# FFN rows transposed by VectorE, normalised by GpSimd, silu on ScalarE, and another order of products at the end of a pair of blocks

## The chip, the cores and the metric

One core of one Trainium2 chip runs the whole program. The metric is the device time of one execution in microseconds; the time of a kernel is the median of its runs.

## The reference

A gated cross-attention block and a gated feed-forward block, each with a residual. x is 2 x 1024 x 512, the context 2 x 77 x 512, there are 16 heads of 32, and the FFN has 1536 hidden units with integer weights scaled by 1/127.

```python
def _silu(x):
    return jax.nn.silu(x)

def _L0_ffn_ref(x, w_gate, w_up, w_down):
    wg = _dequant(w_gate, x.dtype)
    wu = _dequant(w_up, x.dtype)
    wd = _dequant(w_down, x.dtype)
    gate = jnp.einsum('bsd,hd->bsh', x, wg)
    up = jnp.einsum('bsd,hd->bsh', x, wu)
    h = _silu(gate) * up
    return jnp.einsum('bsh,dh->bsd', h, wd)

x = x + jnp.tanh(g_xattn[0]) * _L0_xattn_ref(_layernorm(x, axis=-1), ctx_1024, ctx_1024, ...)
x = x + jnp.tanh(g_ffn[0]) * _L0_ffn_ref(_layernorm(x, axis=-1), ...)
```

## The kernel before, in words

The 2048 rows are eight blocks of 512. A first stage does the attention block by block and stores x_mid in HBM; GpSimd builds beside it the weights' variants w_var (four sums and three plain quarters per slice of 128 hidden units), which go to HBM too. The second stage, to which the change belongs, is the FFN. It takes the blocks in four pairs, p = 0 to 3.

A pair has twelve slots, m = 0 to 11, one per slice of hidden units. In a slot gate and up of both blocks of the pair come from seven products instead of eight (a scheme of Strassen's kind): the quarters A of the weights stand against the quarters B11, B21, B22 and the differences T1 to T4 of the transposed, normalised rows. Each product is 4 matmuls (`strassen`, L1880), since every row variant is held as a rounded part and a remainder (xv[:, j, 0] and xv[:, j, 1]). The slot's weights lie in a ring of three (`load_w`, L385). ScalarE takes three snapshots of partial sums (`snap1`, `snap2`, `snap3`, L973 to L985) and two tanh (L991, L998); VectorE forms the gate and up of both blocks (`gate2`, `upper1`, `upper2`, L1421 to L1456), completes silu by (tanh + 1) x gate (`silu1`, `silu2`, L1435 and L1441) and multiplies (`hidden1`, `hidden2`, L1448 and L1463). ScalarE then rounds the hidden values (`h_high`, L1005) and GpSimd writes the remainder (`h_low`, L705, first th1, then c12).

The down projection (`down`, L1930) of six slots runs behind slot m = 6 for the first half and behind the last slot for the second. One tile of rows takes 12 matmuls, six slots x two parts, and the eight tiles of a pair alternate between two PSUM banks; VectorE adds each to acc (`result`, L1471) and so frees the bank. In `pair` of TensorE the last slot's p4 and p3 and parts of the first two tiles stand before the rest.

The rows of the next pair are prepared during a pair. SyncE loads x2 in four parts in slots 0 to 3 (L361). VectorE takes statistics (`stats2`, L1257) between the first half's results and normalises there (`normalise2`, L1265); GpSimd computes the standard deviations (L654, L656). At the pair's end TensorE transposes the rows in four groups of eight (`turn`, L1704) into PSUM; from there ScalarE and VectorE form B11 to B22 and T1 to T4 (`xv_copy`, `form`, `xv_low`) and GpSimd the remainders of T1 to T4 (L663). For pair 0 the same happens at the end of the attention, where GpSimd normalises (L682).

Every engine runs its own list in the order in which it is written; semaphores tie the lists. An engine that waits holds up all that is behind it in its list. The order of the FFN is in the five functions named `pair`, one per engine. VectorE also takes the maximum of the ring's weights (`largest_gu`, L1476), in slots 0 to 5 of pair 0 and 6 to 11 of the last pair; it decides at the end whether an exact slow path has to run, which it does not here.

## Time and profile before

| | us |
|---|---|
| median of 3 runs | 872.54 |
| lowest and highest | 872.40, 872.73 |
| the profiled execution | 872.86 |
| its span, first to last instruction | 871.0 |

The profile is of one execution. Its span is 1.9 us shorter than the time of the same execution. A timeline row gives the start, the duration of the group, the engine, the line and the operands; an idle time before the group and what ended it stand in brackets. PE is TensorE, DVE VectorE, ACT ScalarE, POOL GpSimd. A matmul's own duration (some 390 ns) overlaps with its neighbours', so the spacing of starts tells what one costs.

### The profile page before, as it was taken

The page shows a single profiled execution, that of the slowest core. Times are in us where ns is not written, and L with a number is a line of the kernel's source. Part 1 is how long each engine was busy: PE and PEld are TensorE (multiplying, and loading weights), DVE is VectorE, ACT ScalarE, POOL GpSimd, SP SyncE. Part 2 cuts the span into 40 slices and gives each one's busy share as a digit, 9 for nine tenths or more (in the row PEclk, how much of TensorE's full clock was granted, in tenths as well). Part 3 has the DMA queues.
Part 4 walks back from the last instruction along what each step waited for, and adds up shares of the span by engine and source line. Part 5 has one row for each costly group of instructions (what it writes and reads, how often), then busy time and mean ns, then how long its engine had stood idle before and what let it go on. Part 6 is the DMA issues. An engine that isn't in the chain of part 4 may idle for free.

```text
span 871.0 us, 12870 instructions
## 1 busy us (share of the span) xinstructions
PE 855.0 (98%) x4087; PEld 706.8 (81%) x4087; DVE 653.3 (75%) x1081; ACT 461.1 (53%) x1130; POOL 403.1 (46%) x344
## 2 busy tenths in 40 slices
PE   8999999999999999999999999999999999999997
PEld 6678888888888887888888888888888888888876
DVE  5988877777786878679688478788487887587882
ACT  5787575756666757546056265165363364461550
POOL 4664555555565665437144444155253256151250
PEclk9999999999999999999999999999999999999999
DMA  9233847272728131567333256043275143243202
GB/s 329 78 107 121 270 153 253 84 241 85 242 97 277 48 133 38 212 234 266 116 120 135 97 187 248 14 165 122 74 247 187 48 164 107 96 171 117 90 38 98
DMA packets 60406, 128.73 MB, mean 148 GB/s; under 512 B 7616, under 2 KB 20416, under 8 KB 60352
## 3 DMA queue, kind: packets, MB, share of 16 engines
q1 hardware_dynamic: 58960, 125.95, 41.9%
q10 hardware_dynamic: 1392, 2.10, 0.7%
q8 instruction: 29, 0.48, 0.2%
q14 instruction: 25, 0.20, 0.1%
HBM read 99.93 MB, written 27.79 MB: 147 GB/s over the span
## 4 chain that ended last, share of the span: by engine, by line
PE 86%; DVE 6%; ACT 3%; issue 1%; DMA 1%; POOL 1%; ACTq 0%; DVEq 0%
PE psum L1880 34%; PE psum L1591 20%; PE psum L1930 18%; PE psum L1660 9%; PE psum L1616 4%; DMA xs<-x_t 1%; PE psum L1704 1%; ACT e L800 1%; POOL hT L705 1%; DVE bn L1055 1%; DVE K L1149 1%; DVE mx L1105 1%; DVE e L1097 0%; DVE qT L1079 0%; DVE mx L1094 0%
## 5 line engine op out<-in xcount | busy, mean ns | idle before, releaser
L1880 PE MATMUL psum<-xv,ring 128*128 128x512 f32 x1344 | 308.0, 390 | 1.0 <-ACT a L985 0.7
L1880 PEld LDWEIGHTS psum<-xv,ring 128*128 128x128 f32 x1344 | 251.3, 188 | 55.1 <-ACT a L985 1.1
L705 POOL TENSOR_TENSOR hT<-th,hT 128x512 fp32r<-128x512 f32 x48 | 86.7, 1806 | 200.7 <-ACT hT L1005 200.7
L1930 PE MATMUL psum<-w_d,hT 128*128 128x512 f32 x768 | 177.7, 390 | 1.3 <-POOL hT L705 0.8
L1930 PEld LDWEIGHTS psum<-w_d,hT 128*128 128x128 f32 x768 | 143.6, 188 | 32.7 <-POOL hT L705 2.0
L554 POOL TENSOR_TENSOR e<-e,rden 128x616 f32<-128x616 f32 x64 | 78.0, 1219 | 110.4 <-DVE rden L1131 75.2
L800 ACT ACTIVATE e<-psum,nmx,q_scale 128x77 f32<-128x77 f32 x256 | 102.9, 428 | 3.1 <-DVE nmx L1111 3.1
L973 ACT ACTIVATE a<-psum 128x512 f32<-128x512 f32 x48 | 28.7, 599 | 131.6 <-PE psum L1880 131.4
L1471 DVE SCALAR_TENSOR_TENSOR acc<-psum,gate_ffn,acc 128x512 f32<-128x512 f32 x64 | 47.6, 749 | 65.1 <-PE psum L1930 65.1
L1660 PE MATMUL psum<-wo,aT 128*128 128x512 f32 x384 | 95.5, 398 | 0.5 <-DVE aT L1079 0.5
L1591 PE MATMUL psum<-xT,wq 128*128 128x512 f32 x360 | 89.1, 398 | 0.4 <-DVE qT L1079 0.4
L1660 PEld LDWEIGHTS psum<-wo,aT 128*128 128x128 f32 x384 | 69.8, 188 | 14.3 <-DVE aT L1079 0.8
L1591 PEld LDWEIGHTS psum<-xT,wq 128*128 128x128 f32 x360 | 65.5, 188 | 14.7 <-DVE qT L1079 1.9
L705 POOL TENSOR_TENSOR hT<-c,hT 128x512 fp32r<-128x512 f32 x48 | 62.3, 1297 | 22.2 <-ACT hT L1005 22.2
L1591 PE MATMUL psum<-pT,V 128*128 128x512 f32 x288 | 68.0, 392 | 0.6 <-DVE aT L1079 0.6
L773 ACT ACTIVATE pT<-psum 128x512 fp32r<-128x512 f32 (+1 forms) x96 | 49.7, 534 | 33.9 <-PE psum L1616 33.9
L1591 PE MATMUL psum<-K,qT 128*128 128x308 f32 x384 | 63.9, 310 | 0.9 <-ACT e L800 0.9
L1591 PEld LDWEIGHTS psum<-pT,V 128*128 128x128 f32 x288 | 53.3, 188 | 12.5 <-DVE aT L1079 1.1
L1435 DVE SCALAR_TENSOR_TENSOR th<-th,c 128x512 f32<-128x512 f32 x48 | 56.1, 1168 | 7.1 <-ACT th L998 4.3
L1591 PEld LDWEIGHTS psum<-K,qT 128*128 128x128 f32 x384 | 56.9, 188 | 5.4 <-ACT e L800 1.8
L1005 ACT ACTIVATE hT<-th 128x512 fp32r<-128x512 f32 x48 | 30.4, 633 | 54.2 <-DVE th L1448 54.2
L1068 DVE TENSOR_TENSOR pT<-psum,pT 128x512 fp32r<-128x512 f32 (+1 forms) x96 | 55.7, 588 | 2.6 <-ACT pT L773 0.9
(110 smaller groups left out, 1204.7 us busy)
## 6 DMA issues: line engine op xcount, KB each, us to landing
ring<-w_var SPq DMA_DIRECT2D x48, 896.0 KB, 4.6
w_var<-stage SPq DMA_DIRECT2D x12, 896.0 KB, 4.6
x_ln<-x SPq DMA_DIRECT2D x32, 256.0 KB, 4.7
x_res<-x SPq DMA_DIRECT2D x32, 256.0 KB, 5.2
x_mid<-x_res SPq DMA_DIRECT2D x32, 256.0 KB, 2.0
x<-x_mid SPq DMA_DIRECT2D x16, 512.0 KB, 5.6
acc<-x_mid SPq DMA_DIRECT2D x16, 512.0 KB, 6.2
out<-acc SPq DMA_DIRECT2D x32, 256.0 KB, 2.0
```

What stands on the lines that cost most here:

```text
L554: nc.gpsimd.tensor_tensor(e[:, t % 2, hs], e[:, t % 2, hs], rden[:, t % 2, hs].unsqueeze(2).to_broadcast([P, UH, SK]), ALU.mult).then_inc( ...
L705: nc.gpsimd.tensor_tensor(hT[:, 1, i % HH, j, :], h[:, :], hT[:, 0, i % HH, j, :].bitcast(f32), ALU.subtract).then_inc(h_lo, 1)
L773: nc.scalar.activation(dst, src, ACT.Copy).then_inc(t_hi, 1)
L800: last = nc.scalar.activation(e[:, t % 2, UH + h, :], s_bank[1][:, h // HG, (h % HG) * SK:(h % HG + 1) * SK], ACT.Exp, bias=nmx[:, t % 2, ...
L1068: nc.vector.tensor_tensor(dst, src, hi.bitcast(f32), ALU.subtract).then_inc(t_free, 1)
L1435: nc.vector.scalar_tensor_tensor(th2[:, :], th2[:, :], 1.0, c22[:, :], ALU.add, ALU.mult)\
L1471: nc.vector.scalar_tensor_tensor(acc[:, t, :], m_bank[t % 2][:, :], gate_ffn[:, 0:1], acc[:, t, :], ALU.mult, ALU.add).then_inc(m_free, 1)
L1591: last = nc.tensor.matmul(dst, stat, mov, start=(j == 0), stop=(j == len(terms) - 1))
L1616: last = nc.tensor.transpose(t_bank[at % 2][:, j * P:(j + 1) * P], rows[:, start:start + P], ident[:, :])
L1660: last = nc.tensor.matmul(m_bank[t % 2][:, :], aT[:, a, m, t * P:(t + 1) * P], wo[:, c, m, :], start=m == 0 and a + c == 0, stop=m == G - ...
L1880: last = nc.tensor.matmul(psum[:, bank, :], stat, mov, start=start and j == 0, stop=j == len(terms) - 1, skip_group_check=not start)
L1930: last = nc.tensor.matmul(m_bank[t % 2][:, :], hT[:, a, m, t // TT, (t % TT) * P:(t % TT + 1) * P], w_d[:, HH * h + m, :], start=m == 0 an ...
```

## The change

Rows and their transposition: for pairs 1 to 3 SyncE loads all four parts of x2 at once, for pair 1 before the last block of the attention is stored, for pairs 2 and 3 at the start of the pair before. VectorE takes the statistics in slots 1 to 4, GpSimd normalises behind its subtractions of slots 3 and 4, and VectorE transposes the rows in 32 operations per pair (`turn_rows`), each of sixteen 32 x 32 squares, from x2 to two new buffers x2_t0 and x2_t1 in SBUF. Of these, 2 stand in slot 5, 2 in slot 6, 20 between the first half's results, 8 in slots 7 to 9. T1 and T3 are formed in slots 10 and 11, T2 and T4 between the second half's results. T1 to T4 take the place of x2. Pair 0 is prepared as before, with TensorE.

silu is one operation on ScalarE, ACT.Silu in the place of ACT.Tanh; VectorE's `silu1` and `silu2` are gone, and so is the factor 0.5 in the gate.

The end of a pair on TensorE: tile 0's slots 0 to 3, p4, tile 1's, p3, tile 2's, then slot 4 of all three, slot 5 of all three, then tiles 3 to 7. Tile 2 is summed in a bank of the gate and up products (set_c[0]). The ring's maxima are all taken in the last pair. The buffer causal moves to a region of the attention, 32 elements are put in front of the ring, and region_b grows.

```diff
-            b12 = sb("b12", [P, KH, TB], f32, b2)
-            sb("gap2", [P, 2 * G * GK + 2 * NV * P - PT * D - KH * TB], f32, b2)
+            x2_t1 = sb("x2_t1", [P, KD, TB], f32, b2)
+            sb("gap2", [P, ALIGN], f32, b2)
             ring = sb("ring", [P, 3, 7, KH, P], f32r, b2)
+            x2_t0 = sb("x2_t0", [P, KD, TB], f32, b2)
...
+        formed_rows = x2[:, :, :].rearrange("p (v k) n -> p v k n", v=TT)
+        b11, b21 = x2_t0[:, 0:KH, :], x2_t0[:, KH:KD, :]
+        b12, b22 = x2_t1[:, 0:KH, :], x2_t1[:, KH:KD, :]
...
+                if rows_ahead:
+                    sp.wait_ge(xb_full, nth(TURNED, 0, B21))
+                    for j in range(TT):
+                        load_x2(1, j)
...
+                if 0 < p < NP - 1:
+                    sp.wait_ge(xv_lo, nth(LO_ORDER, p, T4))
+                    for j in range(TT):
+                        load_x2(p + 1, j)
                 for m in range(MH):
                     i = MH * p + m
                     sp.wait_ge(p3_full, i + 1)
-                    if p == 0 and m < HH:
-                        sp.wait_ge(w_max_done, m + 1)
...
-                    if p + 1 < NP and m < TT:
-                        sp.wait_ge(xb_full, nth(TURNED, p, B21))
-                        load_x2(p + 1, m)
...
+                    if p + 1 < NP and m in (2, 4):
+                        rstd_ahead(2 * p + 1 + m // 2)
+                        mean_ahead(2 * p + 1 + m // 2)
+                    if p + 1 < NP and m in (3, 4):
+                        normalise(2 * p - 1 + m)
                 if p + 1 < NP:
-                    variants_low(p + 1)
+                    for j in LO_ORDER:
+                        xv_low(p + 1, j, j)
...
+            def xv_round(q, j):
+
+                full, half_of = {B11: (b11, 0), B21: (b21, 0), B22: (b22, 1)}[j]
+                act.wait_ge(x2_turned, turned(half_of, q))
+                act.wait_ge(last_use(j), MH * q)
...
-                nc.scalar.activation(th1[:, :], psum[:, set_a[i % 2], :], ACT.Tanh, scale=0.5 * W_SCALE)\
-                    .then_inc(tanh1_done, 1)
-
-            def tanh2(i):
+                nc.scalar.activation(th1[:, :], psum[:, set_a[i % 2], :], ACT.Silu, scale=W_SCALE)\
+                    .then_inc(silu1_done, 1)
...
-                    xv_copy(p + 1, B11, b11_at)
-                tanh2(last)
-                tanh1(last)
+                    xv_round(p + 1, B11)
+                silu2(last)
+                silu1(last)
                 if more:
-                    b12_copy(p + 1)
+                    xv_high(p + 1, T1)
                 h_high(last, 0)
+                if more:
+                    xv_round(p + 1, B21)
                 h_high(last, 1)
                 if more:
-                    xv_high(p + 1, T1)
-                    xv_copy(p + 1, B21, b21_at)
+                    xv_high(p + 1, T3)
                     xv_high(p + 1, T2)
-                    xv_high(p + 1, T3)
                     xv_high(p + 1, T4)
-                    b22_copy(p + 1)
+                    xv_round(p + 1, B22)
...
-            def normalise2(i, tiles=range(TT)):
-                dve.wait_ge(rstd2_ready, i + 1)
-                for t in tiles:
-                    at = TT * (i % 2) + t
-                    nc.vector.tensor_scalar(x2[:, at, :], x2[:, at, :], mv2[:, at, 0:1], rstd2[:, at:at + 1],
-                                            ALU.subtract, ALU.mult).then_inc(x2_normed, 1)
+            def turn_rows(q, half_of, ops):
+
+                tiles = slice(TT * half_of, TT * half_of + TT)
+                dve.wait_ge(x2_normed, PT * q + TT * (half_of + 1))
+                if q > 1:
+                    dve.wait_ge(xb_lo, nth(XB_ORDER, q - 1, B22))
+                for op in ops:
+                    a, c = divmod(op, HG)
+                    rows = x2[a * HD:(a + 1) * HD, tiles, :].rearrange("p t (k n) -> p t k n", n=P)
+                    to = x2_t[half_of][c * HD:(c + 1) * HD].rearrange("p k (t n) -> p t k n", n=P)
+                    nc.vector.transpose(to[:, :, :, a * HD:(a + 1) * HD], rows[:, :, :, c * HD:(c + 1) * HD])\
+                        .then_inc(x2_turned, 1)
...
+                    one, other = b12, b11 if q else pair_of(b11_at)
                 if j == T2:
-                    dve.wait_ge(xb_full, nth(TURNED, q, B22))
-                    dve.wait_ge(v_formed, nth(FORMED, q, T1))
-                    ins = nc.vector.tensor_tensor(lo, pair_of(b22_at), xy[:, T1, 1], ALU.subtract)
+                    one, other = b22 if q else pair_of(b22_at), variant(q, T1)
                 if j == T3:
-                    ins = nc.vector.tensor_tensor(lo, pair_of(b22_at), b12[:, :, :], ALU.subtract)
+                    one, other = b22 if q else pair_of(b22_at), b12
                 if j == T4:
-                    dve.wait_ge(xb_full, nth(TURNED, q, B21))
-                    dve.wait_ge(v_formed, nth(FORMED, q, T2))
-                    ins = nc.vector.tensor_tensor(lo, pair_of(b21_at), xy[:, T2, 1], ALU.subtract)
-                ins.then_inc(v_formed, 1)
+                    one, other = b21 if q else pair_of(b21_at), variant(q, T2)
+                nc.vector.tensor_tensor(variant(q, j), one, other, ALU.subtract).then_inc(v_formed, 1)
...
-            def silu2(i):
-
-                dve.wait_ge(tanh2_done, i + 1)
-                nc.vector.scalar_tensor_tensor(th2[:, :], th2[:, :], 1.0, c22[:, :], ALU.add, ALU.mult)\
-                    .then_inc(silu2_done, 1)
-
-            def silu1(i):
-
-                dve.wait_ge(tanh1_done, i + 1)
-                nc.vector.scalar_tensor_tensor(th1[:, :], th1[:, :], 1.0, psum[:, set_a[i % 2], :],
-                                               ALU.add, ALU.mult).then_inc(silu1_done, 1)
...
+            FILL = (4, 6, 8, 11, 13, 16, 18, 21, 24)
+
             def first_half(p, more):
                 for t in range(PT):
-                    if more:
-                        stats2(2 * p + 2 + t // TT, t % TT)
-                    elif t < HH:
+                    if not more and t < HH:
                         dve.wait_ge(rd_used, HH)
                         largest(MH + t, w_d[:, 2 * t:2 * t + 2, :].bitcast(f32).rearrange("p m d -> p (m d)"))
                     result(p, 0, t)
-                    if more and t >= PT - 2:
-                        normalise2(2 * p + 2, range(2 * (t - PT + 2), 2 * (t - PT + 2) + 2))
-                if more:
-                    normalise2(2 * p + 3)
+                    if more:
+                        turns(p + 1, range(FILL[t], FILL[t + 1]))
...
-                        silu2(i - 1)
-                        silu1(i - 1)
                         hidden1(i - 1)
                         upper2(i - 1)
                         hidden2(i - 1)
-                    if p == 0 and m < HH or p == NP - 1 and m >= HH:
+                    if p == NP - 1:
                         largest_gu(i)
+                    if more and 1 <= m <= TT:
+                        for t in (2 * m - 2, 2 * m - 1):
+                            stats2(2 * p + 2 + t // TT, t % TT)
+                    if more and m in (HH - 1, HH):
+                        turns(p + 1, range(2 * (m - HH + 1), 2 * (m - HH + 2)))
+                    if more and HH < m < HH + 4:
+                        at = (24, 27, 30, 32)[m - HH - 1:m - HH + 1]
+                        turns(p + 1, range(at[0], at[1]))
+                    if more and m == MH - 2:
+                        form(p + 1, T1)
+                    if more and m == MH - 1:
+                        form(p + 1, T3)
                 gate2(last)
-                silu2(last)
                 if more:
                     xv_low(p + 1, B11, b11_at)
-                silu1(last)
                 hidden1(last)
                 upper2(last)
                 hidden2(last)
                 if not more:
                     widest()
-                if more:
-                    form(p + 1, T1)
                 result(p, 1, 0)
                 result(p, 1, 1)
+                result(p, 1, 2)
                 if more:
                     form(p + 1, T2)
-                    form(p + 1, T3)
-                result(p, 1, 2)
-                if more:
                     xv_low(p + 1, B21, b21_at)
-                    form(p + 1, T4)
                 result(p, 1, 3)
                 if more:
+                    form(p + 1, T4)
+                result(p, 1, 4)
+                if more:
                     xv_low(p + 1, B22, b22_at)
-                for t in range(4, PT):
+                for t in range(5, PT):
...
+                    if (h, t) == (1, 2):
+                        pe.wait_ge(c12_done, MH * p + MH - 1)
+                    else:
+                        m_wait(i)
                 h_lo = (h1_lo, h2_lo)[t // TT]
                 for m in slots:
-                    if t % TT == 0:
+                    if t in (0, 1, 2, TT):
...
-                if more:
-                    turn(p + 1, B11)
-                    turn(p + 1, B12)
+                early, late = range(HH - 2), range(HH - 2, HH - 1)
+                down(p, 1, 0, early)
                 p4(last)
+                down(p, 1, 1, early)
                 p3(last)
-                down(p, 1, 0, range(HH - 1))
-                down(p, 1, 1, range(HH - 1))
+                down(p, 1, 2, early)
+                for t in range(3):
+                    down(p, 1, t, late)
                 if not more:
                     pe.wait_ge(w_top_done, 1)
                     pe.wait_ge(c11_done, last)
                     nc.tensor.transpose(psum[0:1, set_b[0], 0:P], w_top[:, :], ident[:, :]).then_inc(w_top_row, 1)
-                down(p, 1, 0, range(HH - 1, HH))
-                down(p, 1, 1, range(HH - 1, HH))
-                if more:
-                    turn(p + 1, B22)
-                    turn(p + 1, B21)
-                for t in range(2, PT):
+                for t in range(3):
+                    down(p, 1, t, range(HH - 1, HH))
+                for t in range(3, PT):
                     down(p, 1, t)
```

## Rows read from the trace of the kernel before

**Rows 1.** The page's part 1: engine, busy us, share of the span, instructions.
```profile
PE 855.0 (98%) x4087; PEld 706.8 (81%) x4087; DVE 653.3 (75%) x1081; ACT 461.1 (53%) x1130; POOL 403.1 (46%) x344
```

**Rows 2.** The chain that ended last, FFN: start us, us, engine, line, count.
```profile
372.00 42.81 PE psum L1880 x188
...
436.58 31.75 PE psum L1880 x140
...
496.02 42.75 PE psum L1880 x188
```

**Rows 3.** Timeline, end of pair 0: start us, us, engine, line, out<-in, count [idle before].
```profile
468.16 1.91 PE L1704 MATMUL psum<-ident,x 128*128 128x128 f32 x16
...
471.74 4.70 PE L1930 MATMUL psum<-w_d,hT 128*128 128x512 f32 x20
...
474.84 1.81 POOL L705 TENSOR_TENSOR hT<-th,hT 128x512 fp32r<-128x512 f32 x1 [3.75 <-ACT hT L1005]
...
476.70 1.20 PE L1930 MATMUL psum<-w_d,hT 128*128 128x512 f32 x4 [0.26 <-POOL hT L705]
...
477.73 1.91 PE L1704 MATMUL psum<-ident,x 128*128 128x128 f32 x16
...
495.85 4.37 PE L1880 MATMUL psum<-xv,ring 128*128 128x512 f32 x18
```

**Rows 4.** Timeline, end of the last pair.
```profile
837.76 2.43 PE L1880 MATMUL psum<-xv,ring 128*128 128x512 f32 x10
...
847.97 1.17 PE L1930 MATMUL psum<-w_d,hT 128*128 128x512 f32 x4
...
848.84 1.41 DVE L1471 SCALAR_TENSOR_TENSOR acc<-psum,gate_ffn,acc 128x512 f32<-128x512 f32 x2
...
849.64 16.61 PE L1930 MATMUL psum<-w_d,hT 128*128 128x512 f32 x72 [0.50 <-DVE acc L1471]
```

**Rows 5.** Timeline of pair 0 around the first-half down projection.
```profile
409.87 0.68 DVE L1430 TENSOR_TENSOR c<-psum,a 128x512 f32<-128x512 f32 x1
...
410.60 1.30 POOL L705 TENSOR_TENSOR hT<-c,hT 128x512 fp32r<-128x512 f32 x1 [0.61 <-ACT hT L1005]
...
414.65 21.93 PE L1930 MATMUL psum<-w_d,hT 128*128 128x512 f32 x96
```

**Rows 6.** Groups by line and form: out<-in, count | busy us, mean ns | idle before.
```profile
L705 POOL TENSOR_TENSOR hT<-th,hT 128x512 fp32r<-128x512 f32 x48 | 86.7, 1806 | 200.7 <-ACT hT L1005 200.7
...
L1660 PE MATMUL psum<-wo,aT 128*128 128x512 f32 x384 | 95.5, 398 | 0.5 <-DVE aT L1079 0.5
...
L1591 PE MATMUL psum<-pT,V 128*128 128x512 f32 x288 | 68.0, 392 | 0.6 <-DVE aT L1079 0.6
...
L705 POOL TENSOR_TENSOR hT<-c,hT 128x512 fp32r<-128x512 f32 x48 | 62.3, 1297 | 22.2 <-ACT hT L1005 22.2
...
L1435 DVE SCALAR_TENSOR_TENSOR th<-th,c 128x512 f32<-128x512 f32 x48 | 56.1, 1168 | 7.1 <-ACT th L998 4.3
...
L1441 DVE SCALAR_TENSOR_TENSOR th<-th,psum 128x512 f32<-128x512 f32 x48 | 32.5, 676 | 1.2 <-ACT th L991 1.2
...
L1257 DVE BATCH_NORM_STATS2 bn<-x 128x6 f32<-128x512 f32 x32 | 21.9, 684 | 0.0
...
L1265 DVE TENSOR_SCALAR x<-x,mv,rstd 128x512 f32<-128x512 f32 x24 | 11.4, 541 | 0.0
...
L711 POOL CAST w_d<-raw_d 128x1024 fp32r<-128x1024 int32 x6 | 8.9, 1505 | 0.0
...
L656 POOL TENSOR_TENSOR rstd<-rstd,half 128x4 f32<-128x4 f32 x8 | 8.4, 1051 | 0.7
...
L682 POOL TENSOR_SCALAR x<-x,nmean,rstd 128x512 f32<-128x512 f32 x8 | 6.1, 773 | 0.0
...
L654 POOL TENSOR_SCALAR rstd<-mv 128x4 f32<-128x4 f32 x8 | 1.6, 194 | 53.2 <-DVE mv L1259 53.2
...
L750 ACT ACT_TABLE_LOAD x1 | 1.3, 1283 | 4.6 <-issue 4.6
```

More of the change, by code:

```diff
@@ L69, in flamingo_gated_block @@
     FIRST = (2, 3, 0, 1)
+    ALIGN = 32
     PT = 2 * TT
@@ L330, in xv_low_ready, with formed, variant, rounded @@
                 eng.wait_ge(xv_lo, nth(LO_ORDER, q, j))
-        def xv_parts(j):
-            return xv[:, j, 0], xv[:, j, 1], xy[:, j, 1]
+        def formed(q, j):
+            return nth((T1, T3, T2, T4) if q else FORMED, q, j)
+        def variant(q, j):
+            return formed_rows[:, FORMED.index(j)] if q else xy[:, j, 1]
+        def rounded(q, j):
+            return nth((B11, T1, B21, T3, T2, T4, B22) if q else HI_ORDER, q, j)
+        def last_use(j):
+            return {B11: p1_full, B21: p2_full, T4: p4_full, T1: p5_full, T2: p6_full, T3: p7_full, B22: p3_full}[j]
         def pair_of(bank):
             return psum[:, bank:bank + 2, :]
+        TURNS = HG * HG
+        def turned(half, q):
+            return TURNS * (2 * (q - 1) + half + 1)
+        def down_bank(h, t):
+            return psum[:, set_c[0], :] if (h, t) == (1, 2) else m_bank[t % 2][:, :]
         block = ctx.enter_context(nc.Block())
@@ L386, in load_w, with residual @@
                     .then_inc(w_in[i % 3], 16)
-            def residual(n, first=False, ahead=False, keeps=((), ())):
+            def residual(n, first=False, ahead=False, keeps=((), ()), rows_ahead=False):
                 for t in range(TT):
@@ L658, in xv_low, with mean_ahead, normalise @@
             def xv_low(q, j, unread):
-                hi, lo, full = xv_parts(j)
-                pool.wait_ge(xv_hi, nth(HI_ORDER, q, j))
-                pool.wait_ge(v_formed, nth(FORMED, q, unread))
-                nc.gpsimd.tensor_tensor(lo, full, hi.bitcast(f32), ALU.subtract).then_inc(xv_lo, 1)
-            def variants_low(q):
-                xv_low(q, T1, T2)
-                xv_low(q, T3, T3)
-                xv_low(q, T2, T4)
-                xv_low(q, T4, T4)
-            def mean_first(i):
-                c = slice(TT * i, TT * i + TT)
+                pool.wait_ge(xv_hi, rounded(q, j))
+                if not q:
+                    pool.wait_ge(v_formed, nth(FORMED, 0, unread))
+                nc.gpsimd.tensor_tensor(xv[:, j, 1], variant(q, j), xv[:, j, 0].bitcast(f32), ALU.subtract)\
+                    .then_inc(xv_lo, 1)
+            def mean_ahead(i):
+                c = slice(TT * (i % 2), TT * (i % 2) + TT)
                 nc.gpsimd.tensor_scalar(nmean2[:, c], mv2[:, c, 0], -1.0, 0.0, ALU.mult, ALU.add).then_inc(nmean_ready, 1)
-            def normalise_first(i, tiles):
+            def normalise(i, tiles=range(TT)):
                 pool.wait_ge(nmean_ready, i + 1)
@@ L1271, in form @@
+            def form(q, j):
+                if q:
+                    dve.wait_ge(x2_turned, turned(1, q))
+                else:
+                    if j == T1:
+                        dve.wait_ge(b12_kept, 1)
+                    dve.wait_ge(xb_full, nth(TURNED, 0, {T1: B11, T2: B22, T3: B22, T4: B21}[j]))
+                if j == T2:
+                    dve.wait_ge(v_formed, formed(q, T1))
+                if j == T4:
+                    dve.wait_ge(v_formed, formed(q, T2))
                 if j == T1:
-                    dve.wait_ge(b12_kept, q + 1)
@@ L1492, in widest, with turns @@
                 nc.vector.tensor_copy(wide[:, :], wide_f[:, :]).then_inc(wide_ready, 1)
+            def turns(q, ops):
+                for half_of in range(2):
+                    inside = [op - TURNS * half_of for op in ops if op // TURNS == half_of]
+                    if inside:
+                        turn_rows(q, half_of, inside)
+            FILL = (4, 6, 8, 11, 13, 16, 18, 21, 24)
             def first_half(p, more):
                 for t in range(PT):
-                    if more:
-                        stats2(2 * p + 2 + t // TT, t % TT)
-                    elif t < HH:
+                    if not more and t < HH:
                         dve.wait_ge(rd_used, HH)
@@ L1851, in last_step @@
                 o(3, range(G))
-                turn(0, B11)
-                turn(0, B12)
+                turn(B11)
+                turn(B12)
                 p(n, 3, 1)
@@ L1867, in _ @@
                 if m == 1:
-                    turn(0, B22)
-            turn(0, B21)
+                    turn(B22)
+            turn(B21)
             pe.wait_ge(m_free, M_LAST + 4)
```

141 lines of the change are left out of this document (62 added, 79 removed).

## Prediction

> **What bounds the kernel now.** I read the page first: TensorE is busy for 98% of the span, VectorE for 75, GpSimd for 46 [rows 1]. So only what TensorE executes, and what makes it pause, can move the time. Next the chain of work that ended last, in order of time [rows 2]: from 372 us it is the FFN, four pairs of blocks, and inside a pair it is only TensorE. The 140 matmuls of the second half take 31.75 us, 0.2268 us each. A pair holds 336 matmuls of the seven-product scheme and 192 of the down projection, 528 x 0.2268 = 119.75 us, but it lasts 496.02 - 372.00 = 124.02 us. These 4.27 us are what the change can reach per pair. The timeline of the pair's end shows them [rows 3]. Sixteen transposes start at 468.16; the 8 matmuls behind them take 1.81, and the down projection starts at 471.74: 1.77 us for the transposes. Of its first 24 matmuls the last four start only at 476.70, released by GpSimd's subtraction of 474.84, so the group ends at 477.73 instead of 477.18: 0.55 us. Sixteen more transposes follow, and the 72 matmuls left (16.33) end at 495.85: 1.79 us. That is 4.11; 0.16 is left over. The last pair has no transposes, but it waits [rows 4]: its seventh product ends at 837.76 + 10 x 0.2268 = 840.03, and 32 matmuls later (7.26) it should be at 847.29, where the row says 849.64: 2.35 us of waits, on ScalarE's snapshot, on VectorE's gate sum (delayed by a maximum of the ring), and on the first result that frees a bank.
>
> **The change, part by part.** TensorE's transposes leave pairs 0 to 2: 3 x 3.56 = 10.7 us off the path.
>
> The new pair end. TensorE now does 8 down matmuls, p4, 8, p3, 8, then slot 4 (6 matmuls) and slot 5 (6) for three rows of tiles at once. The snapshot for p4 has 1.81 us of matmuls over it where the last pair waited; the gate sum for p3 the same and more. Slot 5 is first wanted 38 matmuls or 8.6 us after the seventh product; before it was wanted 4 matmuls ahead of 477.18, 8.1 us after it. VectorE's two fused multiplies are gone from silu, one of them 1168 ns [rows 6], so the last subtraction comes earlier too. I cost the old waits (0.55 in pairs 0 to 2, 2.35 in the last) at nothing. What is late next is the bank: tile row 3 needs the bank of tile row 1, and thus the second result. In [rows 4] the first result starts 848.84 - 847.97 = 0.87 us behind the first closing product, and two take 1.41. So the bank is free at 2.28, and the six matmuls are done at 1.36: a wait of 0.92, plus a restart (four matmuls from 476.70 take 1.03 to the next start, not 0.91 [rows 3]): 1.04 us in all four pairs. The last has one small transpose more, 0.1.
>
> Normalising on GpSimd. Eight operations a pair of 773 ns [rows 6] go in order between the subtractions that the down projection waits for. In pair 0 of before the second subtraction of slot 4 ends at 410.60 + 1.30 = 411.90, and the down projection starts at 414.65 and wants slot 5 eleven matmuls in, at 416.92 [rows 5]. Now GpSimd has the standard deviation (0.19 + 1.05), the mean (0.19) and about 0.1 between them, 1.5 us, and four normalisations, 3.05, ahead of slot 5's first subtraction: it starts at 416.45 and, at the 1297 ns of the undisturbed form [rows 6], ends at 417.75. TensorE waits 0.85 and restarts for 0.12: 1.0 us in pairs 1 and 2. In pair 0 the six conversions of 1505 ns stand in the same queue in slots 0 to 2; GpSimd works them off except for about 0.45, so 1.4 us there. That is 3.4 us in all. Slots 3 and 4 are split late as well; the silu that waits for that reuse of its buffer stands more than half a slot (3.2 us) behind, so I take nothing.
>
> Turning rows on VectorE. 32 operations a pair of 512 elements on 32 partitions; no row of before shows one. From below, a plain pass over 512 elements costs 541 ns; from above, an engine that fills a block and drains it before the next would need two passes, about 1.2 us. I take the statistics' 684 ns [rows 6], one element at a time in one stream, which it is nearest to. VectorE loses 12 x (1168 + 676) ns of silu a pair [rows 6], 22 us, and gets 32 x 0.69 = 22. Twenty of the 32 stand between the eight results of the first half, at 0.7 a result [rows 4]: 20 x 0.69 + 8 x 0.7 = 19.4 us under 96 matmuls, 21.77 us. They fit, so nothing. In the slots with three of them VectorE comes to the gate sum about 1 us late; it now ends at 410.55 where its product starts 12 matmuls before the down projection, at 411.93 [rows 5], 1.4 us later. Nothing. The forming of four variants reads SBUF instead of PSUM at about the same 1.2 us each, and the first variants are formed before the pair ends, so they are ready sooner than now, where the next pair starts without a wait [rows 2, 3].
>
> SyncE. The four 512 KB loads of rows leave the slots and stand ahead of the pair's ring loads, four issues; for pair 1 they stand ahead of the stores of the attention, which start later than they do. The ring is three slots deep, two of them (56 matmuls, 12.7 us) are in hand. Nothing. The ring's maxima of pair 0 move to the last pair, 1.2 us in a slot that has lost 1.8.
>
> ScalarE computes silu instead of tanh: same count and size. One load of a table, 1283 ns [rows 6], must come before the first silu. It costs from nothing, in ScalarE's idle time (busy 53% [rows 1]), to all of its 1.3 us; nearer the first, 0.2. The trace of before shows that one load was enough for Copy, Exp and Tanh. The Trainium skill (ScalarE: Activation LUTs, What ACT_TABLE_LOAD costs) gives about 2.66 us with the drain for a switch of set; by that the sum would be up to 1.4 us higher, as an estimate; the trace of before shows the load alone.
>
> Placement. By the sizes in the code the ring and the row variants stay at equal places modulo 256 bytes, as before; V and pT, equal before, come to lie 128 bytes apart. No row shows unequal operands of this kind. The 288 matmuls with V take 236 ns each, those with Wo, equal too, 249 [rows 6]; the difference bounds a gain or a loss at 288 x 13 ns = 3.7 us. I take nothing.
>
> **Sum.** Pair 0: 4.27 - 0.16 - 1.4 - 1.04 = 1.7. Pairs 1 and 2: 4.11 - 1.0 - 1.04 = 2.1 each. Last pair: 2.35 - 1.14 = 1.2. Less 0.2: 6.9 us. The profiled execution took 872.86 us (span 871.0 and 1.9 around it) and so comes to 866.0; the median of the runs is 0.3 lower, so 865.7.
>
> **Rivals.**
> 1. GpSimd is not late (its queue keeps ahead, or the stretch between has more room than I give it): the 3.4 us come back, 862.3. For it: GpSimd is busy 46% only [rows 1]. Against it: the order of the queue.
> 2. Turns somewhat dearer, 0.8 to 0.95 us: above 0.8 the first half's VectorE work passes 21.77 us and each 0.1 costs 2 us a pair. 866 to 874.
> 3. The slower side: turns at 1.2 us. Twenty and the results need 29.6 us, 7.8 over, in three pairs 23.5: about 889. It decides from 0.92 us a turn, where 3 x 2.3 us eat the gain. For it: nothing in the trace says that blocks overlap. Against it: the one-source rows of 512 elements lie between 0.54 and 0.77 [rows 6].
> 4. Placement costs the whole bound: 869.4.
> 5. The change does not do what it says: silu and the copies between need different tables, so that 1.28 us is paid several times a slot. Four switches are 5.1 us a slot of 28 matmuls or 6.35 us, of which ScalarE's 53% [rows 1] are 3.4: 8.5, 2.1 over, in 44 slots 92 us, some 958. Against it: copies ran between Exp and Tanh on one load.
> 6. Both of GpSimd's sums disturbed by VectorE (its first subtraction takes 1806 ns instead of 1297 [rows 6], once a pair in the stretch before slot 5): 1.5 us more, 867.2.
>
> **How the numbers follow.** Forecast 0.47; rival 1 0.16; 2 0.10; 3 0.08; 4 0.06; 5 0.03; 6 0.10. About 0.2% (1.7 us) is what a measurement of this kernel can tell from no change. Faster: all of the forecast, 1, 4, 6 and half of 2, 0.84. Same: 0.04 from 2. Slower: 3, 5 and the rest of 2, 0.12. The range goes from 861.0 (rival 1 with a gain in placement) to 870.5 (rival 4, most of 2); what lies above is rivals 3, 5 and the end of 2.
>
> **What would show it.** In the changed profile: no transposes on TensorE after 372 us; a turn on VectorE at 0.65 to 0.75 us; a wait of TensorE on GpSimd's hT of about 1 us at the start of the first-half down projection in pairs 0 to 2 (1.4 in pair 0), and one of about 0.9 on VectorE's acc in each pair's end; pairs of about 122.0 us; one more table load; matmul spacing still 0.2268. Matmul spacing away from that, turns over 0.8 us, or waits of TensorE on gate sums would make it wrong.

## The result, and the profile after

The changed kernel takes 878.57 us (median of 4 runs, 878.46 to 878.72), the kernel before in the same session 872.47: a ratio of 1.0070, with a 95% interval of 1.0056 to 1.0084. It is 6.1 us slower, where I had forecast 6.9 us faster; the result lies outside my range. The profiled execution has a span of 876.6 us, 5.6 more than the 871.0 of before.

First line of the page, as in [rows 1]:

```profile
PE 850.1 (97%) x3991; PEld 695.9 (79%) x3991; DVE 662.9 (76%) x1057; ACT 457.5 (52%) x1128; POOL 412.5 (47%) x374
```

TensorE has lost its 96 transposes and is busy 4.9 us less, but its share has fallen: it waits more. The chain in order of time, the starts of the four pairs, as in [rows 2]:

```profile
372.97 24.68 PE psum L1909 x108
...
499.31 24.62 PE psum L1909 x108
...
625.23 24.62 PE psum L1909 x108
...
751.16 42.74 PE psum L1909 x188
...
815.66 31.73 PE psum L1909 x140
```

The attention ends 0.97 us later. The first three pairs last 126.34, 125.92 and 125.93 us. In the kernel before the first lasted 124.02 us, and two later starts in its chain give 123.96 for each of the next two:

```profile
619.98 42.75 PE psum L1880 x188
...
743.94 42.75 PE psum L1880 x188
```

So each of these pairs is 2.0 to 2.3 us longer, not some 2 us shorter. Only the last pair is shorter, 125.44 (876.6 - 751.16) for 127.06 (871.0 - 743.94). A matmul still takes 31.73 / 140 = 0.2266 us. In sum 0.97 + 2.32 + 1.96 + 1.97 - 1.62 = 5.6, the whole difference.

TensorE's waits in the FFN, by what ended them: total us, times, longest:

```profile
PE psum L1962 <- DVE acc L1509: 8.7, 12, 1.6
PE psum L1962 <- POOL hT L734: 4.2, 3, 1.4
PE psum L1909 <- DVE c L1480: 0.5, 3, 0.2
```

The second and the third line are each one wait a pair in pairs 0 to 2. The first line is the surprise: I had expected one such wait at a pair's end, and in pairs 0 to 2 there are four. The timeline of TensorE at the end of pair 1:

```profile
602.99 4.70 PE L1962 MATMUL psum<-w_d,hT 128*128 128x512 f32 x20
608.28 5.74 PE L1962 MATMUL psum<-w_d,hT 128*128 128x512 f32 x24 [0.60 <-DVE acc L1509]
614.22 3.03 PE L1962 MATMUL psum<-w_d,hT 128*128 128x512 f32 x12 [0.20 <-DVE acc L1509]
617.56 3.01 PE L1962 MATMUL psum<-w_d,hT 128*128 128x512 f32 x12 [0.31 <-DVE acc L1509]
622.22 3.01 PE L1962 MATMUL psum<-w_d,hT 128*128 128x512 f32 x12 [1.65 <-DVE acc L1509]
```

By the starts of the matmuls, less their spacing of 0.227, the four pauses with their restarts (the second matmul behind a wait comes 0.11 us late) are 0.87, 0.47, 0.58 and 1.92 us, 3.84 together. The first is the bank reuse of my prediction (1.04). The other 2.97 us stand in no term of it. VectorE in the same stretch, and behind it GpSimd:

```profile
608.80 1.35 DVE L1334 TENSOR_TENSOR x<-x_t,x 128x1024 f32<-128x1024 f32 x1
610.07 3.43 DVE L1340 TENSOR_TENSOR xv<-x_t,xv 128x1024 fp32r<-128x1024 f32 x1
613.43 0.74 DVE L1509 SCALAR_TENSOR_TENSOR acc<-psum,gate_ffn,acc 128x512 f32<-128x512 f32 x1
614.09 2.75 DVE L1334 TENSOR_TENSOR x<-x_t,x 128x1024 f32<-128x1024 f32 x1
616.76 0.74 DVE L1509 SCALAR_TENSOR_TENSOR acc<-psum,gate_ffn,acc 128x512 f32<-128x512 f32 x1
618.92 2.59 DVE L1340 TENSOR_TENSOR xv<-x_t,xv 128x1024 fp32r<-128x1024 f32 x1 [1.41 <-ACT xv L974]
621.43 1.40 DVE L1509 SCALAR_TENSOR_TENSOR acc<-psum,gate_ffn,acc 128x512 f32<-128x512 f32 x2
```

```profile
606.67 2.40 POOL L694 TENSOR_TENSOR xv<-x,xv 128x1024 fp32r<-128x1024 f32 x1
...
606.67 5.75 POOL L694 TENSOR_TENSOR xv<-x,xv 128x1024 fp32r<-128x1024 f32 x2
...
606.67 9.08 POOL L694 TENSOR_TENSOR xv<-x,xv 128x1024 fp32r<-128x1024 f32 x3
...
618.01 2.41 POOL L694 TENSOR_TENSOR xv<-x,xv 128x1024 fp32r<-128x1024 f32 x1 [2.25 <-ACT xv L981]
```

The first three rows of GpSimd are its first subtraction alone, its first two, and its first three together. A subtraction of VectorE that takes 1.2 us from PSUM takes up to 3.43 us here. Read both engines together: GpSimd's second subtraction ends at 606.67 + 5.75 = 612.42, and VectorE's for B21 ends at 613.50, about one undisturbed 1.2 us later. GpSimd's third ends at 615.75, and VectorE's forming of T4 at 616.84, again 1.1 later. GpSimd's fourth ends at 620.42, VectorE's for B22 at 621.51. GpSimd's own second and third take 3.4 and 3.3 us instead of 2.4 in their turn. The two engines do not run side by side, they alternate, a whole instruction each, and the recorded length holds the wait. VectorE's accumulation at 613.43, which reads one operand from PSUM, takes its usual 0.74 us beside GpSimd's third subtraction. The kernel before shows the same at its pair's end: there the subtraction for B21 had one operand in PSUM, and neither engine slowed the other.

```profile
480.18 4.90 POOL L663 TENSOR_TENSOR xv<-xy,xv 128x1024 fp32r<-128x1024 f32 x2 [2.27 <-DVE xy L1278]
...
483.12 1.21 DVE L1290 TENSOR_TENSOR xv<-psum,xv 128x1024 fp32r<-128x1024 f32 x1
```

The rule is one I could have used: the Trainium skill (SBUF — State Buffer, the section on its two separate sides) says that a VectorE instruction with two SBUF inputs and a GpSimd instruction that reads SBUF take turns on a shared port pair, and that the one that starts first holds it for its whole length. The alternation above agrees.

Results 3 to 5 stand behind these operations, and each frees the bank that TensorE needs two tile rows later: the last row starts at 622.22 because result 5 is over only at 621.43 + 0.74 = 622.17.

The queue of GpSimd ahead of slot 5 of pair 1 (the normalisations of slot 3, those of slot 4, and slot 5's first subtraction), and TensorE behind it:

```profile
532.78 3.98 POOL L708 TENSOR_SCALAR x<-x,nmean,rstd 128x512 f32<-128x512 f32 x4
...
540.98 3.47 POOL L708 TENSOR_SCALAR x<-x,nmean,rstd 128x512 f32<-128x512 f32 x4
544.42 1.25 POOL L734 TENSOR_TENSOR hT<-th,hT 128x512 fp32r<-128x512 f32 x1
```

```profile
545.73 14.58 PE L1962 MATMUL psum<-w_d,hT 128*128 128x512 f32 x63 [1.39 <-POOL hT L734]
```

This is the predicted stall, in the predicted place, but with its restart it is 1.66 us, not 1.0.

### The profile page after: what moved, and what is told of

Read it like the earlier page. It is cut to its first block, busy times and chain, and to the rows that moved or that the text cites. A ratio compares the mean times of both kernels' runs of the same rounds, so it can differ in the third digit from the quotient of the medians.

```text
span 876.6 us, 12718 instructions
## 1 busy us (share of the span) xinstructions
PE 850.1 (97%) x3991; PEld 695.9 (79%) x3991; DVE 662.9 (76%) x1057; ACT 457.5 (52%) x1128; POOL 412.5 (47%) x374
## 4 chain that ended last, share of the span: by engine, by line
PE 75%; DVE 10%; POOL 7%; issue 5%; ACT 2%; DVEq 0%; POOLq 0%; ACTq 0%
PE psum L1909 27%; PE psum L1635 20%; PE psum L1962 15%; PE psum L1704 9%; PE psum L1660 4%; POOL hT L734 3%; POOL x L708 3%; DVE x L1334 1%; DVE acc L1509 1%; DVE x_t L1311 1%; ACT e L832 1%; POOL rstd L687 1%; DVE bn L1095 1%; PE psum L1745 1%; DVE K L1189 1%
## 5 line engine op out<-in xcount | busy, mean ns | idle before, releaser
L1909 PE MATMUL psum<-xv,ring 128*128 128x512 f32 x1344 | 309.1, 390 | 0.5 <-DVE c L1480 0.5
L1962 PE MATMUL psum<-w_d,hT 128*128 128x512 f32 x768 | 181.7, 392 | 13.0 <-DVE acc L1509 8.7
L734 POOL TENSOR_TENSOR hT<-th,hT 128x512 fp32r<-128x512 f32 x48 | 67.4, 1404 | 204.8 <-ACT hT L1045 204.8
L1013 ACT ACTIVATE a<-psum 128x512 f32<-128x512 f32 x48 | 28.7, 598 | 130.7 <-PE psum L1909 130.7
L1704 PE MATMUL psum<-wo,aT 128*128 128x512 f32 x384 | 95.4, 398 | 0.5 <-DVE aT L1119 0.5
L1311 DVE STREAM_TRANSPOSE x_t<-x 32x512 f32<-32x512 f32 x96 | 67.4, 702 | 5.6 <-POOL x L708 2.8
L1025 ACT ACTIVATE a<-psum 128x512 f32<-128x512 f32 x48 | 28.7, 599 | 58.2 <-PE psum L1909 58.2
L1501 DVE TENSOR_TENSOR c<-c,th 128x512 f32<-128x512 f32 x48 | 54.4, 1133 | 5.0
```

What stands on the lines that cost most here:

```text
L734: nc.gpsimd.tensor_tensor(hT[:, 1, i % HH, j, :], h[:, :], hT[:, 0, i % HH, j, :].bitcast(f32), ALU.subtract).then_inc(h_lo, 1)
L1311: nc.vector.transpose(to[:, :, :, a * HD:(a + 1) * HD], rows[:, :, :, c * HD:(c + 1) * HD])\
L1501: nc.vector.tensor_tensor(c12[:, :], c12[:, :], th2[:, :], ALU.mult).then_inc(h2_done, 1)
L1704: last = nc.tensor.matmul(m_bank[t % 2][:, :], aT[:, a, m, t * P:(t + 1) * P], wo[:, c, m, :], start=m == 0 and a + c == 0, stop=m == G - ...
L1909: last = nc.tensor.matmul(psum[:, bank, :], stat, mov, start=start and j == 0, stop=j == len(terms) - 1, skip_group_check=not start)
L1962: last = nc.tensor.matmul(down_bank(h, t), hT[:, a, m, t // TT, (t % TT) * P:(t % TT + 1) * P], w_d[:, HH * h + m, :], start=m == 0 and a ...
```

## The experiments

**1. Results first at the pair's end.**

```diff
                 result(p, 1, 2)
                 if more:
                     form(p + 1, T2)
-                    xv_low(p + 1, B21, b21_at)
                 result(p, 1, 3)
                 if more:
-                    form(p + 1, T4)
+                    xv_low(p + 1, B21, b21_at)
                 result(p, 1, 4)
+                if more:
+                    form(p + 1, T4)
+                result(p, 1, 5)
                 if more:
                     xv_low(p + 1, B22, b22_at)
```

> The changed kernel with one edit: at a pair's end VectorE takes result 3 ahead of the subtraction for B21, result 4 ahead of the forming of T4, and result 5 ahead of the subtraction for B22. In the changed kernel TensorE waits there four times on VectorE's accumulation, 0.87, 0.47, 0.58 and 1.92 us, 3.84 in all, and the forming and the two subtractions take 2.7, 3.4 and 2.6 us instead of the 1.2 that I had priced. Theory A (these operations are slowed by GpSimd's subtractions of the same time and stand ahead of the results that free a bank): only the first wait, 0.9 us, stays; three pairs win 2.9 us each, some 8.7, so 869.9 us. The operations themselves stay slow (2.5 to 3.4 us). Rival B (the three-bank order of TensorE is too tight for the results even at their normal length, so that the wait only moves): less than 1 us a pair, 875.5 or more. Rival C (the variants come so late that the next pair's start waits for them): as many microseconds come back as a wait on xv at the pair's start.

Measured: 869.35 us (868.9 to 869.64), 0.9961 of the kernel before (0.9947 to 0.9974): faster than both. TensorE's timeline at the end of pair 1, then VectorE's:

```profile
605.17 13.91 PE L1964 MATMUL psum<-w_d,hT 128*128 128x512 f32 x60 [0.60 <-DVE acc L1509]
```

```profile
608.91 1.48 DVE L1340 TENSOR_TENSOR xv<-x_t,xv 128x1024 fp32r<-128x1024 f32 x1
...
611.63 2.11 DVE L1334 TENSOR_TENSOR x<-x_t,x 128x1024 f32<-128x1024 f32 x1
```

One wait is left, sixty matmuls follow without another, and the next pair starts without one, so rivals B and C fall. I was partly wrong about the lengths: two of the three long operations became shorter (1.48 and 2.11 us, while the last stayed at 2.59), since a subtraction of GpSimd is already part done when VectorE comes to them from a result.

**2. Without GpSimd's four subtractions.**

```diff
                     for j in LO_ORDER:
-                        xv_low(p + 1, j, j)
+                        pool.wait_ge(xv_hi, rounded(p + 1, j))
+                        pool.sem_inc(xv_lo, 1)
```

> The changed kernel, leaving out GpSimd's four subtractions for T1 to T4 in pairs 1 to 3 (the low halves of the four variants are not computed; the counts are still raised). Everything else stands in its order. Theory A (VectorE's two-source operations on SBUF are slowed by GpSimd's at the same time): the forming of T2 and T4 and the subtractions for B21 and B22 return from 1.35, 2.75, 3.4 and 2.6 us to 1.25 each, TensorE's waits on the accumulation fall from 3.84 to about 0.9 us a pair, and the time to about 870 us. Rival D (these operations are slow for another reason, the placement or the loads of rows at this time): they stay at 2.6 to 3.4 us and the time at 878.5.

The kernel leaves out these subtractions and computes no remainders of T1 to T4 in pairs 1 to 3; the semaphore counts are still raised. Measured: 869.21 us (868.85 to 869.28). VectorE's timeline at the end of pair 1, in the order of the changed kernel:

```profile
606.73 1.22 DVE L1341 TENSOR_TENSOR xv<-x_t,xv 128x1024 fp32r<-128x1024 f32 x1
...
608.84 1.22 DVE L1335 TENSOR_TENSOR x<-x_t,x 128x1024 f32<-128x1024 f32 x1
...
612.12 1.23 DVE L1341 TENSOR_TENSOR xv<-x_t,xv 128x1024 fp32r<-128x1024 f32 x1 [0.48 <-ACT xv L975]
```

The same operations on the same addresses, the forming of T2 ahead of them too, take 1.22 us (the last 1.23) once GpSimd is silent, and the same three waits are gone. So GpSimd is what slows them, not the placement or a load (rival D). The two experiments agree within 0.2 us: 9.2 to 9.4 us of the time stood in the three late results of pairs 0 to 2.

**3. V and pT back at like places**, and the reverse on the kernel before. The edit is the same in both, 128 bytes of padding; it moves pT and what is allocated behind it, and V stays.

```diff
+        sb("pad", [P, ALIGN])
         with ExitStack() as c0:
             wq_stage = sb("wq_stage", [P, KD, D], f32, c0)
```

> The changed kernel with 128 bytes of padding ahead of pT, so that V and pT lie at equal places modulo 256 bytes, as before the change. In the changed kernel the spacing of the matmuls with V is 228 to 240 ns where it was 226 to 227, and the FFN begins 0.97 us later (372.97 against 372.00). If the placement is the cause: the spacing goes back to 226 to 227, the FFN begins at 372.0, and the time is 1.0 us less, 877.6. If something else in the attention is (the place of causal, the order of the instructions): no difference in either.

> The kernel before, with 128 bytes of padding ahead of pT: V at 224 and pT at 96 modulo 256 bytes, where both are at 224. The reverse of the run with like places: 1.5 us more than the kernel before, 874.0, with the busy time of the 288 matmuls with V at 69.4 us instead of 68.0. No change would mean that the 1.5 us of that run had another cause.

Measured: 877.04 us (876.57 to 877.23), 1.5 less than the changed kernel; and 873.89 on the kernel before (873.09 to 874.54, ratio 1.0013, 1.0004 to 1.0022), 1.4 more. The group of matmuls with V, first in the changed kernel, then with the padding in it, then in the kernel before with V and pT apart:

```profile
L1635 PE MATMUL psum<-pT,V 128*128 128x512 f32 x288 | 69.4, 396 | 0.4 <-DVE aT L1119 0.4
```

```profile
L1636 PE MATMUL psum<-pT,V 128*128 128x512 f32 x288 | 68.0, 392 | 0.6 <-DVE aT L1120 0.6
```

```profile
L1592 PE MATMUL psum<-pT,V 128*128 128x512 f32 x288 | 69.4, 397 | 0.4 <-DVE aT L1080 0.4
```

Both ways 1.4 us over 288 matmuls, 5 ns each. The padding also moves both operands of the matmuls with Wo, which stay at like places to each other; their group is busy 95.4 us with and without it, so the move itself costs nothing. The FFN now begins at 371.29, 1.7 us earlier than in the changed kernel and 0.7 earlier than before the change, so the 372.0 that I expected was off: one profile places the attention's end only within some tenths, which may be why 0.97 and not 1.4 showed there.

**4. The weight ring and xv at unlike places.**

```diff
-            sb("gap2", [P, ALIGN], f32, b2)
             ring = sb("ring", [P, 3, 7, KH, P], f32r, b2)
+            sb("gap2", [P, ALIGN], f32, b2)
```

> The changed kernel with its 128 bytes of gap behind the weight ring instead of ahead of it: ring at 0 and xv at 128 modulo 256 bytes, where the changed kernel has 128 and 128. V and pT, at 0 and 128, cost 1.4 to 1.5 us over 288 matmuls (69.4 against 68.0 us busy, and the time of the kernel with them at like places was 1.5 us less), 5 ns a matmul. If that is a property of unlike places wherever both operands are streamed from SBUF in this way, the 1344 matmuls of the seven products take 5 ns more each, 6.7 us: 885.3, and their spacing is 228 to 240 instead of 226 to 228. If it is peculiar to V and pT: no change, 878.5 within 0.5.

Measured: 885.27 us (884.26 to 885.99), 6.7 more than the changed kernel. The group of the seven products is busy 309.1 us in the changed kernel, and here:

```profile
L1909 PE MATMUL psum<-xv,ring 128*128 128x512 f32 x1344 | 315.8, 395 | 0.0
```

6.7 us over 1344 matmuls is 5.0 ns each, as with V. That the time, too, rose by just the 6.7 us of the expectation is partly luck. The profiled execution has a span 7.6 us longer: 6.0 in the FFN, where shorter waits give some back (on GpSimd's hT 3.8 us for 4.2, on the gate sum none for 0.5), and 1.6 ahead of it. The edit moves nothing that is used there, and the trace shows another cause. From 12.20 to 15.60 us TensorE had a granted clock of 0.50 (1.2 GHz) in this execution and got through 15 matmuls, where the changed kernel had 1.00 (2.4 GHz) and 23; here it had waited 1.98 us for the load of wk_stage just before. Half the clock for 3.4 us can cost up to 1.7 us. The changed kernel first, then this one:

```profile
12.20:15.60 3.40, 3.40 (x23) 3.07 (x21) 3.40 (x7) 3.06 (x8) 0.00 (x0) 1.00 1.00 349
```

```profile
12.20:15.60 3.40, 3.40 (x15) 3.39 (x14) 1.68 (x4) 2.12 (x5) 0.00 (x0) 0.50 0.98 339
```

Two of the four runs, the profiled one among them, have a mean clock of 0.997 and take 885.9 and 886.0 us; the two at 0.999 take 884.3 and 884.6, 5.9 more than the changed kernel. So unlike places of ring and xv would cost 6.7 us of TensorE's work and about 6 us of time, and both kernels are spared it.

**5. The second block normalised behind slot 5.**

```diff
-                    if p + 1 < NP and m in (3, 4):
-                        normalise(2 * p - 1 + m)
+                    if p + 1 < NP and m in (3, 5):
+                        normalise(2 * p + (m == 5) + 2)
```

> The changed kernel with one edit: GpSimd normalises the second block of rows behind both subtractions of slot 5 instead of behind those of slot 4. In the changed kernel TensorE waits 1.6 to 1.7 us once a pair on GpSimd's hT, eleven matmuls into the first-half down projection. If that wait is GpSimd's queue as I worked it out: it goes wholly (four normalisations of 0.9 us leave the way), three pairs win 1.65 each, 5.0 us, and the time is 873.6. VectorE needs the second block's rows for turn 16 only in the sixth result of the first half, 13 us later, so no new wait there. Rival: part of it comes back, because the first four normalisations in slot 3 already make the queue late: a rest of 0.5 us or more a pair, 875 or above.

Measured: 873.04 us (872.85 to 875.05), 5.5 less than the changed kernel. GpSimd's timeline in pair 1, and TensorE behind it:

```profile
539.79 1.81 POOL L734 TENSOR_TENSOR hT<-th,hT 128x512 fp32r<-128x512 f32 x1 [0.69 <-ACT hT L1045]
...
542.85 3.01 POOL L708 TENSOR_SCALAR x<-x,nmean,rstd 128x512 f32<-128x512 f32 x4
```

```profile
540.29 21.76 PE psum L1962 x96
```

(The last line is a step of the chain.) Slot 5's first subtraction now starts after an idle 0.69 us, and all 96 matmuls of the down projection run through. The whole wait was the queue, and the four normalisations of slot 3 alone do not make it late.

**6. The three edits together.**

> The three edits that won alone, together: results first at the pair's end (878.57 - 869.35 = 9.2 us), V and pT at like places (1.5), the second block normalised behind the subtractions of slot 5 (5.5). They touch different waits. If the three causes are independent, they add up: 16.2 us, 862.3. If one hides another (a later first half leaves the pair's end less room), over 863.5.

Measured: 862.74 us (862.59 to 863.18), 0.4 over the sum and under the 863.5 that would speak for one hiding another. Within what these runs can tell, they are independent.

**7. A fourth bank.** To these edits:

```diff
-            return psum[:, set_c[0], :] if (h, t) == (1, 2) else m_bank[t % 2][:, :]
+            if h and t in (2, 3):
+                return psum[:, (set_c[0], set_b[1])[t - 2], :]
+            return m_bank[t % 2][:, :]
```

with a wait for c11_done of the last slot ahead of row 3.

> As the kernel with three edits, and tile row 3 of the second-half down projection goes to the free gate-sum bank instead of that of tile row 1. The wait that is left at each pair's end is 0.87 us (0.96 in the last). If it is the reuse of row 1's bank: it goes in all four pairs, 3.5 us, 858.8. Rival: it moves to row 4 or row 5, which need the banks of rows 0 and 1: by the rows they are wanted 2.7 us later and are free 0.7 us after, so nothing should be left.

Measured: 859.18 us (858.82 to 860.89), 3.6 less. TensorE's timeline at the end of pair 0:

```profile
473.56 18.31 PE L1969 MATMUL psum<-w_d,hT 128*128 128x512 f32 x80
```

Eighty matmuls without a wait: the 0.87 us was the reuse of row 1's bank, and the wait did not move elsewhere.

**8. Two more turns in the first half.** To that kernel:

```diff
-            FILL = (4, 6, 8, 11, 13, 16, 18, 21, 24)
+            FILL = (4, 7, 9, 12, 15, 17, 20, 23, 26)
-                        at = (24, 27, 30, 32)[m - HH - 1:m - HH + 1]
+                        at = (26, 28, 30, 32)[m - HH - 1:m - HH + 1]
```

> As the kernel with the fourth bank, and two more turns of rows stand between the results of the first half, so that no slot behind it has more than two (before up to three). The pause of TensorE for the gate sum in the slot behind three turns, 0.44 us in each of three pairs, goes: 1.3 us, 857.5. Against it: the first half then has 22 turns and 8 results, 22 x 0.72 + 8 x 0.66 = 21.1 us under 21.77 us of matmuls; if turns are disturbed there to over 0.75, TensorE waits for results instead, and the time is 859 or more.

Measured: 858.40 us (857.59 to 859.7), 0.9841 of the kernel before (0.9827 to 0.9854). Why the gate sum was late, in the changed kernel, GpSimd and VectorE in pair 1:

```profile
570.84 1.29 POOL L734 TENSOR_TENSOR hT<-th,hT 128x512 fp32r<-128x512 f32 x1 [23.91 <-ACT hT L1045]
...
570.89 1.78 DVE L1501 TENSOR_TENSOR c<-c,th 128x512 f32<-128x512 f32 x1
572.71 2.17 DVE L1311 STREAM_TRANSPOSE x_t<-x 32x512 f32<-32x512 f32 x3
574.90 0.69 DVE L1480 TENSOR_TENSOR c<-psum,a 128x512 f32<-128x512 f32 x1
```

The gate sum starts right behind three turns and a product that takes 1.78 us instead of 0.69, because it meets GpSimd's subtraction of 570.84: the product has two sources in SBUF and ends 0.54 us behind it. In the chain of the kernel with the edit the 140 matmuls of the second half, pair 1, are one piece:

```profile
555.83 31.74 PE psum L1914 x140
```

The pause is gone in all three pairs. The gain of 0.8 us is less than the 1.3 of the three pauses, and the ranges of the two kernels overlap, so its size is not settled; the spans differ by 857.0 - 855.6 = 1.4.

**9. The old order at the pair's end, without transposes.** To the kernel of experiment 6:

```diff
-                down(p, 1, 0, early)
                 p4(last)
-                down(p, 1, 1, early)
                 p3(last)
-                down(p, 1, 2, early)
-                for t in range(3):
-                    down(p, 1, t, late)
+                for t in range(2):
+                    down(p, 1, t, range(HH - 1))
```

and rows 0 and 1 alone closed ahead of rows 2 to 7, in two banks.

> As the kernel with three edits (862.74 us), but TensorE's order at a pair's end is that of the kernel before: p4, p3, five slots of tile rows 0 and 1, then their last slots, then rows 2 to 7, with two banks. There are still no transposes. In the kernel before, this order cost 2.35 us of waits in the last pair, where no transposes stood ahead of p4. If the transposes covered these waits in the other pairs, they now appear in all four: about 2.35 a pair in place of the 0.87 to 1.06 of the new order, 4 x 1.4 = 5.5 us, 868.2. If the new order is worth nothing (the waits belonged to the ring's maximum and silu on VectorE): 862.7, or less by the wait for row 1's bank.

Measured: 868.1 us (867.96 to 868.72), 5.4 more. TensorE's timeline at the end of pair 1:

```profile
591.97 1.20 PE L1912 MATMUL psum<-xv,ring 128*128 128x512 f32 x4 [0.69 <-ACT a L1026]
593.42 1.19 PE L1912 MATMUL psum<-xv,ring 128*128 128x512 f32 x4 [0.26 <-DVE c L1481]
...
600.50 3.70 PE L1962 MATMUL psum<-w_d,hT 128*128 128x512 f32 x15 [0.39 <-DVE acc L1510]
```

The three waits that [rows 4] show for the last pair now stand in every pair, with their restarts 2.15 us in pairs 0 to 2 where the kernel before had 0.55. The transposes had covered the rest. Taking the transposes away without the new order would have given 3 x 1.6 = 4.8 of their 10.7 us back.

## Why the prediction was wrong

**The step that failed** is the sentence "The forming of four variants reads SBUF instead of PSUM at about the same 1.2 us each ... so they are ready sooner than now", with the subtractions of VectorE left at their price without a word. From SBUF, beside GpSimd's subtractions, two formings and two subtractions take 1.35, 3.43, 2.75 and 2.59 us, and results 3 to 5 stand behind them. That is 8.8 us of TensorE's time in three pairs by the pauses (2.9 to 3.0 each), 9.2 by experiment 1 and 9.4 by experiment 2. Without it the changed kernel is 3 us faster than before.

The evidence lay in my own rows. [Rows 6] give 1168 ns for the fused multiply of th and c, and 676 for its twin with an operand in PSUM; and 1806 ns for one of GpSimd's subtractions, 1297 for the other. I used the 1806 as an isolated risk (rival 6), and the 1168 as a saving. Two instances in the timeline of the kernel before show what it was:

```profile
379.19 0.68 DVE L1435 SCALAR_TENSOR_TENSOR th<-th,c 128x512 f32<-128x512 f32 x1
...
385.21 1.30 POOL L705 TENSOR_TENSOR hT<-c,hT 128x512 fp32r<-128x512 f32 x1 [1.13 <-ACT hT L1005]
385.69 1.37 DVE L1435 SCALAR_TENSOR_TENSOR th<-th,c 128x512 f32<-128x512 f32 x1
```

At 379.19 GpSimd is idle and it takes 0.68 us; beside GpSimd it takes 1.37. Taking the fused multiplies away did not take the meeting away: the product behind them (the one into c) rose from 696 to 1133 ns, and the conversion's and the first subtraction's means on GpSimd fell (1505 to 1276, 1806 to 1404).

**Point by point.**
- Transposes, 10.7 us off the path: right; the changed profile has none on TensorE in the FFN.
- Bank reuse, 1.04 us a pair: right in place, 0.87 in three pairs and 0.96 in the last (experiment 7). The old waits at nothing: right. The new order is worth more than the sum shows, 5.4 us (experiment 9), because the transposes no longer cover these waits.
- GpSimd's queue: right in place, too small. The stretch ahead of the four normalisations took 1.70 us (539.28 to 540.98), not 1.5, and each of them 0.87, not 0.773. That is 0.6 us a pair; 5.0 us in all for the 3.4 of the sum, 5.5 by experiment 5.
- Turns: 702 ns for the 690 of the forecast, so rivals 2 and 3 fall. (Two passes of 541 ns, from which rival 3 has its 1.2 us, would be 1.08.) "They fit, so nothing" held for the first half. For the slots with three turns I took the gate sum to be 1.4 us early, without the product's meeting with GpSimd: 0.44 us in each of three pairs was lost.
- Placement, taken at nothing with a bound of 3.7 us: 1.4 to 1.5 us, within the bound. The longer 249 ns of the matmuls with Wo that gave it have, then, another cause, as those have like places.
- The table load: two loads in place of one, 1283 ns each. The second starts at 379.25, ScalarE's next operation 1.30 us later, so nothing beyond the load itself is paid, and TensorE shows no pause there. Rival 5 falls.
- SyncE, and the maxima moved to the last pair: no wait of TensorE on either.

The sum with the measured terms, against my -6.9: +8.8 for the late results, +1.6 for the queue, +1.6 for gate sums (three of 0.44, and 0.3 in pair 0 where VectorE waited on a normalisation), +1.0 for the attention, -0.6 for the bank reuse being shorter, -0.2 for the table: +5.3, where the spans differ by 5.6. Where the 0.3 us left lie is open.

None of my rivals named the right place. Rival 6 had the right mechanism, two engines that disturb each other, at the wrong place and at a sixth of its price. For a slower kernel I looked to a dearer turn, whose price no row showed. What made it slower was an operand moved to SBUF, and the price of that stood in a row.

## What to carry to other kernels

When an edit moves an operand of a VectorE instruction from PSUM to SBUF, so that both sources lie in SBUF, price it anew: list what GpSimd executes in the same stretch, and add to each such instruction of VectorE the rest of the GpSimd instruction that it meets. Two forms of one operation with different means, as 1168 and 676 ns here, are worth a look at single instances before either is carried into a sum. At a stage's end, order an engine's queue by who waits: a result that frees a bank goes ahead of preparations for the next stage.

## What the runs showed of the hardware that I had not expected

- VectorE with two SBUF sources and GpSimd alternate whole instructions: 1.22 us becomes 1.35 to 3.43 by how much of GpSimd's is left, and GpSimd's 2.4 becomes 3.4. With one source in PSUM VectorE takes the same either way, 0.74 us for an accumulation and 1.21 for the subtraction of before.
- Matmuls whose two operands lie 128 bytes apart modulo 256 take 5 ns more each, in three comparisons: 1.4 us over 288 with V both ways, 6.7 us of busy time over 1344 with the ring. Which other distances cost this, and why, was not tried.
- The best version measured, with all of experiments 1, 3, 5, 7 and 8, takes 858.4 us: 20.2 us less than the changed kernel, 14.5 less than the 872.9 of the kernel before beside it.
